# Mixture of experts on one core: two units of the first layer, then two of the second

## What is computed

```python
xf = x.reshape(B * S, D)                        # 256 x 512
scores = xf @ Wr + br                           # 256 x 8
_, top_idx = jax.lax.top_k(scores, K)           # K = 2
...
router_weights = jax.nn.softmax(jnp.where(mask, scores, -jnp.inf), axis=-1)
h = jax.nn.gelu(jnp.einsum('td,edp->etp', xf, W1) + b1[:, None, :])   # p = 2048
y = jnp.einsum('etp,epd->etd', h, W2) + b2[:, None, :]
out = jnp.einsum('te,etd->td', router_weights, y)
```

## Time and profile before

| | |
|---|---|
| median of three runs | 1226.79 us (1225.6 to 1227.8) |
| the profiled execution | 1224.32 us, its span 1222.2 us |
| PE busy in the span | 1189.2 us, 97% |
| DVE, ACT busy | 56%, 44% |
| mean granted clock of TensorE | 0.991 |
| experts, from the first matmul of H(0) to PE's last matmul | 848.61 to about 1216.3 us of the span |

### The profile page before, as it was taken

How to read it: one execution, slowest core, us unless ns; L and a number is a source line. 1 busy time by engine, 2 the same in 40 slices (tenths; PEclk the granted TensorE clock), 3 DMA queues, 4 the chain that set the end, 5 groups by cost and what they waited for, 6 DMA issues and landing times. The chain is left out here.

```text
span 1222.2 us, 23053 instructions
## 1 busy us (share of the span) xinstructions
PE 1189.2 (97%) x9712; PEld 954.2 (78%) x9712; DVE 679.2 (56%) x1210; ACT 531.7 (44%) x897; POOL 216.4 (18%) x178
## 2 busy tenths in 40 slices
PE   7999999999999999999899999997999999999998
PEld 6788888888788888865456676864989999999997
DVE  4654544545464534365788873044665665665662
ACT  5432333332333332214389994153644544444441
POOL 2243333434333433350000000010000000000000
PEclk9999999999999999999999999898999999999999
DMA  7210101010100020326313323301544554454440
GB/s 295 69 53 1 65 2 53 1 49 5 36 19 1 27 70 2 131 86 242 136 73 139 139 75 138 134 1 38 204 177 171 205 202 164 184 206 184 166 165 18
DMA packets 28157, 126.01 MB, mean 103 GB/s; under 512 B 2715, under 2 KB 2971, under 8 KB 17572
## 3 DMA queue, kind: packets, MB, share of 16 engines
q1 hardware_dynamic: 28068, 124.74, 27.2%
HBM read 124.20 MB, written 0.52 MB: 102 GB/s over the span
## 5 line engine op out<-in xcount | busy, mean ns | idle before, releaser
L566 POOL TENSOR_TENSOR norm_both<-norm_both,prob 128x512 f32<-128x512 f32 x118 | 154.8, 1312 | 149.2 <-DVE prob L358 141.8
L57 PE MATMUL mo_h_ps<-mo_x_hi,mo_w_hi 128*128 128x256 f32 x512 | 146.7, 286 | 2.1 <-DVE mo_x_lo L1800 2.1
L495 ACT ACTIVATE prob<-u_ps 128x512 f32<-128x512 f32 x128 | 66.1, 606 | 186.4 <-PE u_ps L668 186.4
L58 PE MATMUL mo_h_ps<-mo_x_lo,mo_w_hi 128*128 128x256 f32 x512 | 146.4, 286 | 0.0
L59 PE MATMUL mo_h_ps<-mo_x_hi,mo_w_lo 128*128 128x256 f32 x512 | 146.3, 286 | 0.0
L341 DVE TENSOR_TENSOR turned<-k_ps,tabs 128x512 f32<-128x512 f32 x32 | 22.1, 690 | 195.9 <-PE k_ps L59 195.9
L1754 DVE TENSOR_TENSOR mo_w_lo<-w_raw,mo_w_hi 128x2048 fp32r<-128x2048 f32 x32 | 73.3, 2292 | 73.8 <-ACT mo_w_hi L1703 73.8
L57 PE MATMUL k_ps<-ctx_hi,wk_hi 128*128 128x512 f32 x256 | 104.2, 407 | 0.0
L57 PE MATMUL u_ps<-wv_hi,ctx_hi 128*128 128x512 f32 x256 | 103.1, 403 | 0.8 <-ACT prob L495 0.8
L57 PEld LDWEIGHTS mo_h_ps<-mo_x_hi,mo_w_hi 128*128 128x128 f32 x512 | 99.8, 195 | 3.7 <-DVE mo_x_lo L1800 2.5
L484 ACT ACTIVATE vals<-u_ps 128x512 f32<-128x512 f32 x64 | 38.2, 597 | 145.8 <-PE u_ps L59 145.8
(11 more groups left out here) (264 smaller groups left out, 2297.6 us busy)
## 6 DMA issues: line engine op xcount, KB each, us to landing
w_raw<-in_w SPq DMA_DIRECT2D x64, 1024.0 KB, 6.3
ctx_raw<-in_ctx_rows SPq DMA_DIRECT2D x8, 1024.0 KB, 5.7
x_k<-in_ctx_T SPq DMA_DIRECT2D x8, 1024.0 KB, 7.0
x_val<-in_ctx_heads SPq DMA_DIRECT2D x8, 1024.0 KB, 4.9
tabs<-in_rot_tabs SPq DMA_DIRECT2D x8, 512.0 KB, 4.2
vals<-in_wq_rows SPq DMA_DIRECT2D x4, 512.0 KB, 8.0
ctx_raw<-in_wo SPq DMA_DIRECT2D x1, 2048.0 KB, 9.7
x_mask<-in_mask SPq DMA_DIRECT2D x2, 1024.0 KB, 9.0
```

Source lines behind the costliest of these rows:

```text
L57: pe.matmul(out, w_hi, x_hi, start=start, stop=False)
L58: pe.matmul(out, w_hi, x_lo, start=False, stop=False)
L495: act.activation(prob[:, t % 2, i, :], u_ps[:, i, :], ACT.Exp).then_inc(s["exped"], 1)
L566: ins = pool.tensor_tensor(to, to, src, ALU.add)
```

## The change

Only PE's program is changed. In `expert` the four units are no longer taken as H(U+1), O(U) one by one. Two H come first and then two O: H(U+1), H(U+2), O(U), O(U+1). In the first expert the same is written out by hand, and there `turn_weights` moves from behind H(2) to behind H(3), and `second_bias` from behind H(3) to behind H(4), which is `hidden(1, 0)`. Every matmul stays, with the same operands and the same waits.

```diff
@@ -1929,10 +1929,12 @@
             def expert(e, par, last=False):
-                for j in range(NU):
-                    if not (last and j == NU - 1):
-                        hidden(e, j + 1)
+                for j in (0, 2):
+                    hidden(e, j + 1)
+                    if not (last and j == NU - 2):
+                        hidden(e, j + 2)
                     output(e, j, par)
+                    output(e, j + 1, par)
@@ -1945,14 +1947,14 @@
             hidden(0, 0, first=True)
             logits()
             hidden(0, 1, first=True)
+            hidden(0, 2)
             output(0, 0, 0, first=True)
-            hidden(0, 2)
-            turn_weights()
             output(0, 1, 0, first=True)
             hidden(0, 3)
+            turn_weights()
+            hidden(1, 0)
             second_bias()
             output(0, 2, 0, first=True)
-            hidden(1, 0)
             output(0, 3, 0, first=True)
             pe.wait_ge(s["acc"], NB)
             with pe.Fori(0, E // 2 - 1) as i:
```

## The result

The changed kernel takes 1232.81 us (median of five runs, 1232.3 to 1234.11) against 1227.8 us (1225.6 to 1228.29) for the kernel before: a ratio of 1.0048, 95% interval 1.0033 to 1.0062. It is slower by 5.0 us by the medians and by 5.9 us by the ratio. A second comparison, with 27 runs of the kernel before, gave 1.0046 (1.0032 to 1.0059).

What follows compares the result with a forecast made beforehand. The prediction took PE to bound the kernel. A 5.1 us wait before H(4) plus 2.0 us of low clock made 7.1 us, added to 1226.79 us for 1233.9 us; range 1231.3 to 1236.5 us.

Steps and rivals of the forecast that it cites:

- What the change removes: Passes of PE between H and O, 30 fewer: each worth zero, so 0 us taken.
- other bound (0.5 us): Two O side by side at the end: 0.017 us saved an O, 0.5 us for the kernel.
- Rival (C): Alternating layers slows the matmuls; half the passes gone return 15.2 us, giving 1218.7 us; chance 4%.
- The wait on H(4): First expert: PE starts H(4) at 893.97 in place of 888.88, 5.1 us late; bounds 5.0 and 5.3.
- The chain of 5.13 us: First expert: from the transposes' start through DVE's copy to the end of `low1` of unit 4, 5.13 us.
- handover of 0.1 us: From the end of `low1` of unit 4 on DVE to H(4)'s start on PE: 0.1 us.
- The clock: PE's clock falls to 0.50 in the gap and stays low into H(4): 2.0 us, bounds 1.7 and 2.9.
- Rival (A): The wait on H(4) comes but the clock does not fall: 1231.9 us; chance 5%.
- Behind it: After H(4): later `second_bias` delays `add_bias` and `split` of unit 3, but O(3) starts late enough; cost 0.
- The loop: Second H of each pair has 2.5 us margin for its `low1`; loads arrive in time; cost 0.
- Rival (B): Margin fails through bursts of loads; second H waits in 14 pairs, 7 us more, 1240.9 us; chance 7%.
- The sum: Wait 5.1 plus clock 2.0 is 7.1 us over the kernel before, giving 1233.9 us; bounds 6.7 and 8.2.

Runs made afterwards that it cites:

- The loop alone: Against the kernel before: first expert in the old order, loop in the new order of pairs; measured 1.0003 (0.9995 to 1.0012).

## Why the prediction was right, and where its numbers were off

The forecast was 1233.9 us, 7.1 over the kernel before; 1232.81 us were measured, 5.0 to 5.9 over it. That the time itself is only 1.1 us off is in part luck: the kernel before came out 1.0 us higher in the comparison than the 1226.79 us of the forecast. The difference is too high by 1.2 to 2.1 us, and below the forecast's own bounds of 6.7 to 8.2.

- **What the change removes: nothing.** Right to within 0.3 us. The loop alone gave 1.0003. Its trace and that with the transposes ahead of H(3) (850.71 to 1217.76) have 367.1 us from H(0) to the last matmul in place of 367.3, 0.24 and 0.28 less, and H(0) is equally long in all three. A pair takes 22.42 in place of 22.44 us. So the order in pairs gives the small return that the prediction had as its other bound (0.5 us) and took as 0. Rival (C), 15.2 us, is out: with 26 passes fewer in the loop alone it is 0.01 us a pass, where (C) needed 0.24.
- **The wait on H(4): 5.1 us, measured 4.9.** Right, by the chain named, 0.06 below the lower bound of 5.0. The chain of 5.13 us was 5.02, the handover of 0.1 us was 0.06. `gelu` was early as worked out, and `route_weights` had ended 6 us before. Swapping two lines on PE or moving the copy on DVE each took all of the loss away, so it is this pair of programs and nothing that goes with pairs.
- **The clock: 2.0 us, measured 1.6 to 1.9 in the traces.** The mechanism was right and shown by filling the wait. The size was a little high, and two of three traces, with 1.6, are below the lower bound of 1.7. In one trace the clock fell within the wait and in the other two just behind the start of H(4), so the work had 4.13 or 3.4 us at the low level, not H(0)'s 4.40. H(0) was also not quite the case that the prediction made of it, the same matmuls behind a gap of that length: between its gap of 4.8 us and H(0) stand the eight matmuls of L1940 and a second gap of 2.1 us, and the clock had been low since 842.7, ahead of both. That its 2.0 us came so near is in part luck. Rival (A), no fall, is out: three traces of three have it.

  The Trainium skill ("TensorE: Matmul & The Clock Gate", Part 1) says that the moment at which the clock comes back varies between runs. These traces agree: it was 4.1, 3.5 and 3.7 us after H(4)'s start, behind the same wait.
- **Behind it: 0.** Right: no wait of PE from H(4) to the end.
- **The loop: margin 2.5 us.** Right: 2.2 us more on DVE cost nothing, 3.3 us cost 1.0 us a pair by the starts, which puts the margin that can be used at 2.3; the trace has `low1` done 2.56 us ahead. Rival (B) is out, though its first part was there: ACT waited once for a load, 1.1 us, which the margin of that unit, odd and larger, took up.
- **The sum.** 7.1 us against 6.4 and 6.1 in traces (without H(0)'s part), and 5.6 to 5.9 in times with intervals of 1.7 us to either side. Against the traces the error is that of three terms, all too high for the loss: 0.1 to 0.4 us in the clock, 0.2 in the wait and 0.3 in what pairs give back. The rest of the gap to the times is inside what the runs can tell.

## What to carry to other kernels

When an engine's order is changed, look for the instruction on another engine that waits for what was moved, and then at all that stands behind that one in its queue: here a copy of 0.41 us held up 4.2 us of work, with what the bound engine asked for next at its end. A wait that the trace shows as short (0.83 us) may be the head of a chain that only the old order covered. Where the bound engine never waits, a new order of its work has little to gain (0.3 us here) and uses up margin, so work the margin out before and keep the order that has more.

## What was unexpected

- Behind the four 8-row matmuls of `second_bias` the granted clock fell in all three kernels with added matmuls ahead of H(0) (at 896, 896 and 902 us, for 3.4 us), and in none of the other eleven traces of this study, though the same four matmuls ran behind an H and ahead of O(2) there too. Why was not tested.
- The clock also falls for 3.4 us at a time in the middle of work that no version touches, in other places from one execution to the next (591 and 618 us in the trace after, neither in that before). This makes spans of single traces differ by some 3 us, as much as half of the effect studied here.
